# Mean and inverse deviation of each row made at the end of both zone stages, and read by the next stage

## The chip, the cores and the metric

The kernel runs on one core of a Trainium2 chip. The metric is the device time in microseconds (us) of one launch. Before the change it is 1563.74 us, the median of 3 runs (1562.68 to 1564.3). The profiled execution took 1563.83 us; its span, from the first to the last recorded instruction, is 1562.0 us.

## The reference

32 samples of 256 rows (tokens) with 128 features go through six steps. Each normalises the rows over their features, and adds its result to them:

```
x = x + 0.5 * zones(layernorm(x));  x = x + splat_attention(layernorm(x))
x = x + 0.5 * zones(layernorm(x));  x = x + 0.5 * splines(layernorm(x))
x = x + causal_attention(layernorm(x));  x = x + 0.5 * splines(layernorm(x))
layernorm(x) = (x - mean(x)) / sqrt(var(x) + 1e-5)        # over the 128 features of a row
zones(x)     = x + sum over 8 zones e of w[sample, e] * gelu(x @ Wa[e]) @ Wb[e]
               # w: softmax of a small router on the sample's mean row, the best 3 of 8 kept and rescaled
splines(x)   = (sum_h relu((x @ Win + bin) * W1 + b1) * W2 + b2) @ Wout + bout   # 64 knots, 16 bends each
```

The splat attention has 16 heads of 8 features and softmax over logits that come from 16 Gaussian centers per head. Only the layernorms that stand in front of the splat attention and of the first spline step bear on the change: their mean and 1 / sqrt(var + 1e-5) are two numbers for each row, known as soon as the zone step before has added its result to the row.

## The kernel before

All rows stay in SBUF for the whole launch, in `x_res`: 128 partitions, and for each sample two tiles (`TILES` = 2) of 128 features. The stages follow each other: a start with a first router (`route_a`), `zones_a`, `splat`, a second router (`route_b`), `zones_b`, `spline_a`, `causal`, `spline_b`. Each stage is a block of its own: one program for each engine, written by hand, with semaphores between them; the order of calls in such a program is the order on the engine. A stage begins when all engines have ended the one before (the barrier, L253, shows in the trace as `PEq L253`). Loops take two samples a turn (`pairs`), since buffers alternate.

**Moments of rows.** `RowNorm` (from L93) makes them for one sample in two parts. VectorE does `statistics` (L116 to L128): one `bn_stats` for each tile, then one `bn_aggr` for each, which leaves mean and variance in `moments`. GpSimd does `power` (L130 to L139): it adds eps, then raises to -0.5, which gives `rstd`. `s.mean` and `s.rstd` are tables in SBUF with one column for each tile of rows; stages can leave moments there for the next one. `PairNorm` (from L165) is the same for the two samples of a pair at once, used by the spline stages.

**Zone stages** (`zones`, L735 to L953). The incoming rows' moments are in the tables already. ScalarE normalises the rows (L865), TensorE turns them to features on partitions, ScalarE keeps the high float16 part and VectorE the low one (`keep_low`, L912 to L916). For each of the three chosen zones (k = 0 to 2) TensorE makes the first product (L804 to L806), ScalarE the gelu (L876), VectorE splits it in a high and a low float16 part (`split_unit`, L918 to L926), and TensorE makes the second product (L818 to L820). The sum over the three zones is copied by ScalarE and turned back by TensorE (L827). VectorE adds it to the rows (`add`, L928 to L933). GpSimd has added half of the normalised rows by then (`take_half`, L762 to L770: a product with 0.5 and a sum, 256 columns each). VectorE's order for one sample is this:

```
for k in range(TOP_K):
    split_unit(TOP_K * b + k, b, k)
if turns:
    keep_low(b + 2, parity)
if not is_first:
    add(b - 1, 1 - parity)
```

**Splat stage** (L956 to L1413). 32 samples in slots. It makes the moments of its own incoming rows in `statistics` (L1295 to L1298) on VectorE, four samples ahead, and `norm.power` and `apply` on GpSimd (L1376 to L1386), three ahead; `apply` subtracts the mean and multiplies by rstd. For the router and the zones that follow it also makes the moments of the rows that it has ended, with the same class (`ended`), and copies them into the tables (`keep_moments`, L1388 to L1392). VectorE's main work is the maxima of the logits (L1312).

**First spline stage** (`splines`, from L1417). 16 pairs of samples, 512 columns each. An engine's program is a list of steps with the number of pairs by which each is ahead, written by hand:

```
run(dve, (keep_inner, 1), (apply, 3), (statistics, 4), (add, -1))
run(pool, (bend, 1), (power, 4), (bias, 2))
run(act, (bend_first, 0), (keep_summed, -1), (bend_rest, 0), (keep_normed, 2))
```

`apply` normalises four tiles on VectorE, TensorE turns them (L1518) into `turned`, and `keep_normed` (L1556 to L1561) copies that out of PSUM on ScalarE. TensorE makes the knots' inputs (L1525, L1528), VectorE copies half of them (`keep_inner`, L1474) and bends some (L1477), ScalarE and GpSimd bend the rest, TensorE sums the bends of each knot (L1539), ScalarE copies the sums (`keep_summed`, L1578), and TensorE makes the result, which VectorE adds (L1485). The second spline stage calls the same function.

## Time and profile before

| | us |
|---|---|
| median of 3 runs (range) | 1563.74 (1562.68 to 1564.3) |
| profiled execution, whole | 1563.83 |
| its span | 1562.0 |
| TensorE busy | 1433.0 (92%) |
| VectorE busy | 1202.8 (77%) |
| ScalarE busy | 986.4 (63%) |
| GpSimd busy | 465.3 (30%) |

| stretch of the span | length | TensorE | VectorE | ScalarE | GpSimd |
|---|---|---|---|---|---|
| 61.90 to 331.00, zones_a | 269.10 | 266.88 | 216.97 | 162.49 | 53.28 |
| 335.00 to 917.00, splat | 582.00 | 565.58 | 451.47 | 370.46 | 136.99 |
| 961.00 to 1230.00, zones_b | 269.00 | 267.88 | 216.58 | 160.60 | 51.73 |
| 1231.60 to 1325.00, spline_a | 93.40 | 78.63 | 79.57 | 78.95 | 76.38 |

The times come from one profiled execution, those in the rows below in us from the span's start. PE is TensorE, DVE VectorE, ACT ScalarE, POOL GpSimd, SP SyncE; a "q" behind a name is the engine's sequencer. L with a number is a line of the kernel. An arrow reads "written <- read". In brackets stands how long the engine was idle before the instruction, and what it waited for. Busy shares are means over stages with different limits, so each stage is read by itself.

### The profile page before, as it was taken

How to read it: one execution, taken by the hardware profiler on the slowest of the kernel's cores; microseconds unless marked ns; L12 is line 12 of the kernel's file. 1: busy time of each engine (PE TensorE's matmuls, PEld its weight loads, DVE VectorE, ACT ScalarE, POOL GpSimd, SP SyncE). 2: the span in 40 equal slices, each digit the busy share in tenths (PEclk: the TensorE clock that was granted, in tenths of full speed). 3: DMA queues.
4: the chain of work that ended last, by engine and by line, in shares of the span. 5: the costliest groups of instructions: out<-in, count | busy, mean ns of one | idle time of the engine just before them, and what ended most of it. 6: DMA issues, size and time to landing. Idle time of an engine off the chain costs nothing. (4 is left out here: it accounts for less than half of the span.)

```text
span 1562.0 us, 43828 instructions
## 1 busy us (share of the span) xinstructions
PE 1433.0 (92%) x14442; PEld 1040.8 (67%) x14443; DVE 1202.8 (77%) x2634; ACT 986.4 (63%) x1478; POOL 465.3 (30%) x694
## 2 busy tenths in 40 slices
PE   1699999978999999999999987999999799799697
PEld 1499999955666666666666655999999544699443
DVE  8688888847778887877887854888888697587695
ACT  5366566534666666666666654665665399577597
POOL 6321221211222222222222202211221298222585
PEclk9999999988999999999999998999999899899899
DMA  5000000000000000000000000000000000000011
GB/s 237 1 1 0 0 0 0 0 1 1 2 2 2 1 0 0 0 0 0 0 0 1 2 2 2 1 0 0 0 0 0 1 0 1 1 0 1 8 47 54
DMA packets 9527, 14.40 MB, mean 9 GB/s; under 512 B 368, under 2 KB 8560, under 8 KB 8688
## 3 DMA queue, kind: packets, MB, share of 16 engines
q1 hardware_dynamic: 9456, 13.44, 2.3%
q8 instruction: 46, 0.75, 0.2%
q14 instruction: 25, 0.20, 0.0%
HBM read 9.25 MB, written 4.19 MB: 9 GB/s over the span
## 5 line engine op out<-in xcount | busy, mean ns | idle before, releaser
L1312 DVE TENSOR_REDUCE neg_max<-splat_fill_ps 128x2 f16<-128x512 f32 x512 | 334.0, 691 | 91.0 <-PE splat_fill_ps L1091 87.0
L1237 ACT ACTIVATE splat_probs<-splat_ring 128x1024 f32<-128x1024 f32 x256 | 248.1, 1021 | 98.3 <-PE splat_ring L1118 98.3
L876 ACT ACTIVATE zones_b_hidden<-zones_b_hidden_ps,gelu_scale 128x1024 f32<-128x1024 f32 x96 | 107.1, 1115 | 85.5 <-PE zones_b_hidden_ps L806 84.2
L876 ACT ACTIVATE zones_a_hidden<-zones_a_hidden_ps,gelu_scale 128x1024 f32<-128x1024 f32 x96 | 107.1, 1115 | 84.8 <-PE zones_a_hidden_ps L806 83.5
L1118 PE MATMUL splat_ring<-splat_queries,splat_keys 32*128 32x256 f32 x2048 | 153.0, 393 | 4.2 <-ACT splat_probs L1237 3.2
L1091 PE MATMUL splat_fill_ps<-splat_keys,splat_queries 32*128 32x256 bf16 x1024 | 146.0, 278 | 6.2 <-DVE neg_max L1312 3.3
L1132 PE MATMUL splat_mixed_ps<-splat_probs,values 128*32 128x256 f32 x2048 | 137.0, 385 | 0.4 <-ACT splat_probs L1237 0.4
L925 DVE SCALAR_TENSOR_TENSOR zones_b_hid_lo<-zones_b_hidden,unit_scale,zones_b_hid_hi 128x1024 f16<-128x1024 f32 x96 | 123.6, 1288 | 3.4
L925 DVE SCALAR_TENSOR_TENSOR zones_a_hid_lo<-zones_a_hidden,unit_scale,zones_a_hid_hi 128x1024 f16<-128x1024 f32 x96 | 123.6, 1288 | 3.4
L133 POOL TENSOR_TENSOR splat_ended_shifted<-splat_ended_moments,eps 128x2 f32<-128x2 f32 x32 | 6.3, 197 | 344.4 <-DVE splat_ended_moments L127 344.4
L1118 PEld LDWEIGHTS splat_ring<-splat_queries,splat_keys 32*128 32x128 f32 x2048 | 100.0, 185 | 11.6 <-ACT splat_probs L1237 4.4
L804 PE MATMUL zones_b_hidden_ps<-zones_b_norm_hi,wa_hi 128*128 128x256 f16 x384 | 105.8, 276 | 0.3 <-DVE zones_b_norm_lo L915 0.3
L804 PE MATMUL zones_a_hidden_ps<-zones_a_norm_hi,wa_hi 128*128 128x256 f16 x384 | 105.5, 275 | 0.3 <-DVE zones_a_norm_lo L915 0.3
L805 PE MATMUL zones_b_hidden_ps<-zones_b_norm_lo,wa_hi 128*128 128x256 f16 x384 | 105.8, 275 | 0.0
L806 PE MATMUL zones_b_hidden_ps<-zones_b_norm_hi,wa_lo 128*128 128x256 f16 x384 | 105.7, 275 | 0.0
L818 PE MATMUL zones_a_result_ps<-zones_a_hid_hi,wb_hi 128*128 128x256 f16 x384 | 104.7, 273 | 1.0 <-DVE zones_a_hid_lo L925 1.0
L805 PE MATMUL zones_a_hidden_ps<-zones_a_norm_lo,wa_hi 128*128 128x256 f16 x384 | 105.4, 275 | 0.0
L806 PE MATMUL zones_a_hidden_ps<-zones_a_norm_hi,wa_lo 128*128 128x256 f16 x384 | 105.4, 275 | 0.0
L818 PE MATMUL zones_b_result_ps<-zones_b_hid_hi,wb_hi 128*128 128x256 f16 x384 | 104.7, 273 | 0.6 <-DVE zones_b_hid_lo L925 0.6
L819 PE MATMUL zones_a_result_ps<-zones_a_hid_lo,wb_hi 128*128 128x256 f16 x384 | 104.7, 273 | 0.0
L820 PE MATMUL zones_a_result_ps<-zones_a_hid_hi,wb_lo 128*128 128x256 f16 x384 | 104.7, 273 | 0.0
L819 PE MATMUL zones_b_result_ps<-zones_b_hid_lo,wb_hi 128*128 128x256 f16 x384 | 104.7, 273 | 0.0
(356 smaller groups left out, 3498.3 us busy)
## 6 DMA issues: line engine op xcount, KB each, us to landing
x_res<-rows SPq DMA_DIRECT2D x4, 1024.0 KB, 18.8
out<-x_res SPq DMA_DIRECT2D x16, 256.0 KB, 2.3
stage_a<-wa SPq DMA_DIRECT2D x1, 2048.0 KB, 8.8
stage_b<-wb SPq DMA_DIRECT2D x1, 2048.0 KB, 13.2
packed<-table SPq DMA_DIRECT2D x1, 840.0 KB, 4.4
```

Source lines behind the costliest of these rows:

```text
L804: nc.tensor.matmul(out, s.wa_hi[:, at], x_hi, start=True, stop=False)
L805: nc.tensor.matmul(out, s.wa_hi[:, at], x_lo, start=False, stop=False)
L806: last = nc.tensor.matmul(out, s.wa_lo[:, at], x_hi, start=False, stop=True)
L818: nc.tensor.matmul(out, s.wb_hi[:, at], hi, start=(k == 0 and c == 0), stop=False)
L819: nc.tensor.matmul(out, s.wb_hi[:, at], lo, start=False, stop=False)
L876: nc.scalar.activation(hidden[k][:, :, :], hidden_ps[of][:, :, :], ACT.Gelu_apprx_tanh, scale=s.gelu_scale[:, :]).then_inc(gelu_done, 1)
L925: nc.vector.scalar_tensor_tensor(hid_lo[k][:, :, :], hidden[k][:, :, :], scale, hid_hi[k][:, :, :], ALU.mult, ALU.subtract).then_inc(split, 1)
L1091: last = nc.tensor.matmul(fill_ps[f % 2][:, n, :], upper(queries[at], rows, t + n, slice(tile * P, (tile + 1) * P)), upper(keys[at], rows, ...
L1118: last = nc.tensor.matmul(ring[g // 2][:, 2 * (g % 2) + key_tile, :], keys[at][rows, t, key_tile * P:(key_tile + 1) * P], queries[at][rows ...
L1132: last = nc.tensor.matmul(mixed_ps[head_rows(g), t % 2, :], s.values[:, at, key_tile, HEAD_GROUPS * t + g, :], probs[(2 * t + g // 2) % PR ...
L1237: nc.scalar.activation(probs[u % PROB_BUFFERS][:, :, :, :].rearrange("p h k i -> p (h k) i"), ring[u % 2][:, :, :], ACT.Exp).then_inc(exp_ ...
L1312: nc.vector.tensor_reduce(s.neg_max[:, tile, t:t + 2, GROUP * g + SPLATS], fill_ps[f % 2][:, :, :], AX.X, ALU.max, negate=True).then_inc(m ...
```

## The change

Both zone stages now make the moments of the rows that they have ended. On VectorE each sample b from the third on gets the statistics of sample b - 2 (`end`), between `keep_low` and `add`. GpSimd makes their power and copies mean and rstd into the tables (`keep_moments`), four samples behind, after each halving; the first six halvings stand outside the loop. Behind the last add VectorE does `end` for the last two samples, and GpSimd's last four `keep_moments` follow its last halving. The splat stage loses its own `statistics` and `norm.power`; its `apply` reads the tables. The first spline stage loses `statistics` and `power`; its `apply` reads the tables, one column a tile, and `keep_normed` moves from ScalarE to VectorE. The second spline stage stays as it is.

```diff
-def zones(nc, s, stage):
+def zones(nc, s, stage, moments=False):
...
+        ended = RowNorm(nc, s, ctx, stage + "_ended", 0)
...
-                take_half(0, 0)
-                take_half(1, 1)
-                with pairs(pool, 2, SAMPLES) as i:
+                def keep_moments(b, parity):
+                    ended.power(pool, b, parity)
+                    columns = slice(TILES * b, TILES * (b + 1)) if isinstance(b, int) else bass.ds(b * TILES, TILES)
+                    settle(pool, ended.rstd_ready, b + 1)
+                    nc.gpsimd.tensor_copy(s.mean[:, columns], ended.moments[parity][:, :, 0])
+                    nc.gpsimd.tensor_copy(s.rstd[:, columns], ended.rstd[parity][:, :]).then_inc(ended.ready, 1)
+                for b in range(4):
+                    take_half(b, b % 2)
+                take_half(4, 0)
+                if moments:
+                    keep_moments(0, 0)
+                take_half(5, 1)
+                if moments:
+                    keep_moments(1, 1)
+                with pairs(pool, 6, SAMPLES) as i:
                     for parity in range(2):
                         take_half(i + parity, parity)
+                        if moments:
+                            keep_moments(i + parity - 4, parity)
+                if moments:
+                    for b in range(SAMPLES - 4, SAMPLES):
+                        keep_moments(b, b % 2)
...
+                    if moments and not (isinstance(b, int) and b < 2):
+                        end(b - 2, parity)
                     if not is_first:
                         add(b - 1, 1 - parity)
+                def end(b, parity):
+                    settle(dve, added, b + 1)
+                    settle(dve, ended.ready, b - 1)
+                    ended.statistics(dve, b, parity)
                 keep_low(0, 0)
                 keep_low(1, 1)
                 sample(0, 0, is_first=True)
-                with pairs(dve, 1, LOOP_END) as i:
+                for b in range(1, 5):
+                    sample(b, b % 2)
+                with pairs(dve, 5, LOOP_END) as i:
                     sample(i, 1)
                     sample(i + 1, 0)
                 sample(SAMPLES - 3, 1)
                 sample(SAMPLES - 2, 0, turns=False)
                 sample(SAMPLES - 1, 1, turns=False)
                 add(SAMPLES - 1, 1)
+                if moments:
+                    end(SAMPLES - 2, 0)
+                    end(SAMPLES - 1, 1)
...
-        norm = RowNorm(nc, s, ctx, stage, 1, DEEP)
         ended = RowNorm(nc, s, ctx, stage + "_ended", 0, DEEP)
-        normed, norm_ready = norm.out[0], norm.ready
+        normed, norm_ready = sb(stage + "_normed", [P, TILES, P], F32), sem("norm_ready")
...
-                def statistics(b, at):
-
-                    wait(dve, norm_ready, b - DEEP + 1)
-                    norm.statistics(dve, b, at)
...
-                    if there(b, 4):
-                        statistics(b + 4, after)
...
-                def apply(b, at):
-                    pool.wait_ge(norm.rstd_ready, b + 1)
-                    wait(pool, norm_ready, b)
+                def apply(b):
+                    columns = slice(TILES * b, TILES * (b + 1)) if isinstance(b, int) else bass.ds(b * TILES, TILES)
+                    settle(pool, norm_ready, b)
                     nc.gpsimd.tensor_tensor(centered[:, :, :], tile_of(s.x_res, b),
-                                            norm.moments[at][:, :, 0:1].to_broadcast([P, TILES, P]),
+                                            s.mean[:, columns].unsqueeze(2).to_broadcast([P, TILES, P]),
                                             ALU.subtract).then_inc(centered_ready, 1)
-                    pool.wait_ge(centered_ready, b + 1)
-                    wait(pool, normt_done, b)
+                    settle(pool, centered_ready, b + 1)
+                    settle(pool, normt_done, b)
                     nc.gpsimd.tensor_tensor(normed[:, :, :], centered[:, :, :],
-                                            norm.rstd[at][:, :].unsqueeze(2).to_broadcast([P, TILES, P]),
+                                            s.rstd[:, columns].unsqueeze(2).to_broadcast([P, TILES, P]),
                                             ALU.mult).then_inc(norm_ready, 1)
...
-                        norm.power(pool, b + 3, at)
-                        apply(b + 3, at)
+                        apply(b + 3)
...
+def splines(nc, s, stage, out=None, normed_before=False):
...
-                    norm.apply(dve, p, parity, normed[parity])
+                    if normed_before:
+                        for t in range(PAIR):
+                            column = bass.ds(p * PAIR + t, 1)
+                            last = nc.vector.tensor_scalar(normed[parity][:, t, :], pair_of(s.x_res, p, t),
+                                                           s.mean[:, column], s.rstd[:, column],
+                                                           ALU.subtract, ALU.mult)
+                        last.then_inc(norm_ready, 1)
+                    else:
+                        norm.apply(dve, p, parity, normed[parity])
+                def keep_normed(p, parity):
+                    dve.wait_ge(turned_ready, p + 1)
+                    wait(dve, inner_a_ready, p - 1)
+                    nc.vector.tensor_copy(normed_t[parity][:, :], turned[:, :]).then_inc(normt_ready, 1)
...
-                run(dve, (keep_inner, 1), (apply, 3), (statistics, 4), (add, -1))
+                if normed_before:
+                    run(dve, (keep_inner, 1), (keep_normed, 2), (apply, 3), (add, -1))
+                else:
+                    run(dve, (keep_inner, 1), (apply, 3), (statistics, 4), (add, -1))
...
-                run(pool, (bend, 1), (power, 4), (bias, 2))
+                if normed_before:
+                    run(pool, (bend, 1), (bias, 2))
+                else:
+                    run(pool, (bend, 1), (power, 4), (bias, 2))
...
-                run(act, (bend_first, 0), (keep_summed, -1), (bend_rest, 0), (keep_normed, 2))
+                if normed_before:
+                    run(act, (bend_first, 0), (keep_summed, -1), (bend_rest, 0))
+                else:
+                    run(act, (bend_first, 0), (keep_summed, -1), (bend_rest, 0), (keep_normed, 2))
...
-        zones(nc, s, "zones_a")
+        zones(nc, s, "zones_a", moments=True)
         recycle(nc)
         splat_attention(nc, s, "splat")
         route(nc, s, "route_b")
-        zones(nc, s, "zones_b")
+        zones(nc, s, "zones_b", moments=True)
         recycle(nc)
-        splines(nc, s, "spline_a")
+        splines(nc, s, "spline_a", normed_before=True)
```

In the pieces of the instruction order below, `ISA` and `REGISTER_ALU` are instructions of the engine's sequencer (waits, addresses), and brackets give the semaphores waited for.

**VectorE, loop over samples in zones_a.** Before, from the low part of the unit k = 2 (`hid_lo`) to the add:

```order
L925 SCALAR_TENSOR_TENSOR zones_a_hid_lo<-zones_a_hidden,unit_scale,zones_a_hid_hi 128x1024 [waits zones_a_high]
L914 REGISTER_ALU
L915 TENSOR_TENSOR zones_a_norm_lo<-zones_a_turned,zones_a_norm_hi 128x256 [waits zones_a_norm_high]
L932 ISA [waits zones_a_x_ready,zones_a_turned_ready]
L932 TENSOR_TENSOR x_res<-x_res,zones_a_result_ps 128x256
```

After, from `norm_lo` on (the low part of unit k = 2 stands ahead of it as before):

```order
L936 TENSOR_TENSOR zones_a_norm_lo<-zones_a_turned,zones_a_norm_hi 128x256 [waits zones_a_norm_high]
L71 REGISTER_ALU
L71 REGISTER_ALU [waits zones_a_added]
L63 REGISTER_ALU [waits zones_a_ended_norm_ready]
L120 ISA [waits zones_a_ended_moments_ready]
L120 BN_STATS zones_a_ended_stats<-x_res 128x6
L120 ISA
L120 BN_STATS zones_a_ended_stats<-x_res 128x6
L127 BN_AGGR zones_a_ended_moments<-zones_a_ended_stats 128x2 [waits zones_a_ended_stats_ready]
L127 BN_AGGR zones_a_ended_moments<-zones_a_ended_stats 128x2
L953 ISA [waits zones_a_x_ready,zones_a_turned_ready]
L953 TENSOR_TENSOR x_res<-x_res,zones_a_result_ps 128x256
```

Two `BN_STATS`, two `BN_AGGR` and the waits for `added` and `ended_norm_ready` have come between `norm_lo` and the add to `x_res`.

**GpSimd, loop over samples in zones_a.** Before, one halving and the next:

```order
L774 ISA
L766 TENSOR_TENSOR zones_a_half<-zones_a_normed,half 128x256 [waits zones_a_x_ready,zones_a_norm_ready]
L770 ISA [waits zones_a_half_ready]
L770 TENSOR_TENSOR x_res<-x_res,zones_a_half 128x256
```

After, from the add of one halving to the add of the next, for the second sample of a turn:

```order
L133 TENSOR_TENSOR zones_a_ended_shifted<-zones_a_ended_moments,eps 128x2 [waits zones_a_ended_rstd_ready]
L63 REGISTER_ALU [waits zones_a_ended_shifted_ready]
L137 TENSOR_TENSOR zones_a_ended_rstd<-zones_a_ended_shifted,minus_half 128x2 [waits zones_a_ended_norm_ready]
L778 ISA [waits zones_a_ended_rstd_ready]
L778 COPY mean<-zones_a_ended_moments 128x2
L779 REGISTER_ALU
L779 COPY rstd<-zones_a_ended_rstd 128x2
L766 REGISTER_ALU
L768 TENSOR_TENSOR zones_a_half<-zones_a_normed,half 128x256 [waits zones_a_x_ready,zones_a_norm_ready]
L772 ISA [waits zones_a_half_ready]
L772 TENSOR_TENSOR x_res<-x_res,zones_a_half 128x256
```

Two operations on two columns, with a wait for VectorE's `ended_moments`, and two copies into the tables now stand between two halvings.

**VectorE, start of spline_a.** Before, the first pair's moments, its norm (x3 stands for three more rows alike), and the second pair's:

```order
L183 BN_STATS spline_a_stats<-x_res 128x6 x4
L189 BN_AGGR spline_a_moments<-spline_a_stats 128x2 [waits start_zone_stats_ready]
L189 BN_AGGR spline_a_moments<-spline_a_stats 128x2 x3
L205 TENSOR_SCALAR spline_a_normed<-x_res,spline_a_moments,spline_a_rstd 128x128 [waits start_zone_powered]
L205 TENSOR_SCALAR spline_a_normed<-x_res,spline_a_moments,spline_a_rstd 128x128 x3
L183 BN_STATS spline_a_stats<-x_res 128x6 [waits start_zone_moments_ready]
```

After:

```order
L1495 TENSOR_SCALAR spline_a_normed<-x_res,mean,rstd 128x128 x4
L1505 COPY spline_a_normed_t<-spline_a_turned 128x512 [waits start_packed_loaded]
L1495 TENSOR_SCALAR spline_a_normed<-x_res,mean,rstd 128x128 x4
L1513 COPY spline_a_inner_b<-spline_a_inner_b_ps 128x512 [waits start_masks_ready]
L1516 TENSOR_SCALAR spline_a_bent<-spline_a_inner_b,packed,minus_bias 128x512 [waits start_blank]
L1505 COPY spline_a_normed_t<-spline_a_turned 128x512 [waits start_packed_loaded]
```

The statistics are gone, the norm of the first pair is the stage's first instruction, and the copy of the turned rows (L1505) stands between the norms.

## Rows read from the trace of the kernel before

**Rows 1.** busy time in zones_a: start:end and length, then each engine's busy us (xcount)

```profile
61.90:331.00 269.10, 266.88 (x2418) 238.84 (x2418) 216.97 (x255) 162.49 (x224) 53.28 (x64) 1.00 0.00 0
```

**Rows 2.** timeline, zones_a: start us, length us, engine line op out<-in xcount [idle before]

```profile
91.92 0.42 DVE L932 TENSOR_TENSOR x_res<-x_res,zones_a_result_ps 128x256 f32 x1 [0.82 <-PE zones_a_result_ps L827]
92.55 0.75 DVE L922 TENSOR_SCALAR zones_a_hid_hi<-zones_a_hidden,unit_scale 128x1024 f16<-128x1024 f32 x1 [0.21 <-issue]
93.34 1.28 DVE L925 SCALAR_TENSOR_TENSOR zones_a_hid_lo<-zones_a_hidden,unit_scale,zones_a_hid_hi 128x1024 f16<-128x1024 f32 x1
...
95.53 0.27 PE L818 MATMUL zones_a_result_ps<-zones_a_hid_hi,wb_hi 128*128 128x256 f16 x1
...
98.98 0.42 DVE L915 TENSOR_TENSOR zones_a_norm_lo<-zones_a_turned,zones_a_norm_hi 128x256 f16<-128x256 f32 x1
100.24 0.42 DVE L932 TENSOR_TENSOR x_res<-x_res,zones_a_result_ps 128x256 f32 x1 [0.84 <-PE zones_a_result_ps L827]
```

**Rows 3.** timeline of DVE and POOL: three meetings of the two engines

```profile
97.78 1.28 DVE L925 SCALAR_TENSOR_TENSOR zones_a_hid_lo<-zones_a_hidden,unit_scale,zones_a_hid_hi 128x1024 f16<-128x1024 f32 x1
...
98.57 0.97 POOL L766 TENSOR_TENSOR zones_a_half<-zones_a_normed,half 128x256 f32<-128x256 f32 x1 [6.34 <-ACT zones_a_normed L865]
...
75.35 1.24 POOL L770 TENSOR_TENSOR x_res<-x_res,zones_a_half 128x256 f32 x1 [0.26 <-POOL zones_a_half L766]
76.05 1.63 DVE L925 SCALAR_TENSOR_TENSOR zones_a_hid_lo<-zones_a_hidden,unit_scale,zones_a_hid_hi 128x1024 f16<-128x1024 f32 x1
...
1246.82 1.03 POOL L199 TENSOR_TENSOR spline_a_rstd<-spline_a_shifted,minus_half 128x4 f32<-128x4 f32 x1
1247.15 0.55 DVE L1477 TENSOR_SCALAR spline_a_bent<-spline_a_inner_b,packed,minus_bias 128x512 f32<-128x512 f32 x1
```

**Rows 4.** timeline, splat slot, DVE then POOL: moments of ended rows

```profile
621.03 0.49 DVE L120 BATCH_NORM_STATS2 splat_ended_stats<-x_res 128x6 f32 x2
621.62 0.25 DVE L127 BATCH_NORM_AGGREGATE splat_ended_moments<-splat_ended_stats 128x2 f32<-128x6 f32 x2
621.79 1.26 DVE L1312 TENSOR_REDUCE neg_max<-splat_fill_ps 128x2 f16<-128x512 f32 x2
624.80 1.30 DVE L1312 TENSOR_REDUCE neg_max<-splat_fill_ps 128x2 f16<-128x512 f32 x2 [1.75 <-PE splat_fill_ps L1091]
...
621.95 0.20 POOL L133 TENSOR_TENSOR splat_ended_shifted<-splat_ended_moments,eps 128x2 f32<-128x2 f32 x1 [11.09 <-DVE splat_ended_moments L127]
...
623.27 0.19 POOL L1392 COPY rstd<-splat_ended_rstd 128x2 f32 x1
```

**Rows 5.** timeline, border from zones_a to splat

```profile
333.68 0.42 DVE L932 TENSOR_TENSOR x_res<-x_res,zones_a_result_ps 128x256 f32<-128x256 f32 x1 [2.31 <-PE zones_a_result_ps L827]
335.23 0.49 DVE L120 BATCH_NORM_STATS2 splat_stats<-x_res 128x6 f32<-128x128 f32 x2 [1.13 <-PEq L253]
...
337.55 0.61 POOL L1379 TENSOR_TENSOR splat_centered<-x_res,splat_moments 128x256 f32<-128x256 f32 x1
```

**Rows 6.** timeline, start of spline_a

```profile
1231.62 0.87 DVE L183 BATCH_NORM_STATS2 spline_a_stats<-x_res 128x6 f32<-128x128 f32 x4 [1.15 <-PEq L253]
...
1234.40 1.12 DVE L205 TENSOR_SCALAR spline_a_normed<-x_res,spline_a_moments,spline_a_rstd 128x128 f32<-128x128 f32 x4 [1.42 <-POOL spline_a_rstd L199]
...
1236.72 0.60 ACT L1560 ACTIVATE spline_a_normed_t<-spline_a_turned 128x512 f32<-128x512 f32 x1 [7.20 <-PE spline_a_turned L1518]
...
1238.19 1.12 DVE L205 TENSOR_SCALAR spline_a_normed<-x_res,spline_a_moments,spline_a_rstd 128x128 f32<-128x128 f32 x4 [1.40 <-POOL spline_a_rstd L199]
...
1246.42 0.69 DVE L1474 COPY spline_a_inner_b<-spline_a_inner_b_ps 128x512 f32<-128x512 f32 x1
```

**Rows 7.** timeline of ACT, spline_a: the copies of the knots' sums

```profile
1316.07 0.69 ACT L1578 ACTIVATE spline_a_summed<-spline_a_summed_ps,packed 128x512 f32<-128x512 f32 x1 [0.22 <-PE spline_a_summed_ps L1539]
...
1321.54 0.69 ACT L1578 ACTIVATE spline_a_summed<-spline_a_summed_ps,packed 128x512 f32<-128x512 f32 x1 [0.22 <-PE spline_a_summed_ps L1539]
...
1327.01 0.69 ACT L1578 ACTIVATE spline_a_summed<-spline_a_summed_ps,packed 128x512 f32<-128x512 f32 x1 [0.71 <-PE spline_a_summed_ps L1539]
```

## Prediction: what the change does to the time

> **What bounds the kernel now.** I read the busy time by stage first, then the timelines of one steady sample or pair in each touched stage, then the four borders between stages.
>
> In the zone stages TensorE is the bound: 266.88 of 269.10 us busy in zones_a [rows 1]. VectorE has air there. One sample is 8.32 us long (add to add, 91.92 to 100.24), and before every add VectorE stands idle for 0.82 to 0.84 us, waiting for the result that TensorE turns back [rows 2]. The new work is put into this hole. The next high part of a loop's first sample begins 0.63 after the add (0.21 of it issue); its first low part ends at 94.62 and TensorE asks for it at 95.53, so VectorE may be 0.91 late before TensorE notices [rows 2].
>
> In the splat stage the statistics sit where VectorE is early: two maxima after them it is idle for 1.75 us until TensorE has filled the next [rows 4]. Taking 0.84 us away in front of that idle time makes it longer and nothing else.
>
> In the spline stage the period is not set by ScalarE's sum of work. The copies of the knots' sums start at 1316.07, 1321.54 and 1327.01: two gaps of 5.47 us. The first of these pairs still had the copy of turned rows on ScalarE, the second (near the end, where no pair is left to turn) had not; only the idle time in front of the sums' copy grew, from 0.22 to 0.71 us [rows 7]. The loop that closes is bend, TensorE's knot sums, their copy, bend; the copy that the change moves to VectorE is not in it.
>
> **The change part by part.**
>
> *Statistics in the zone loops (+).* Word for word the splat stage does the same: two statistics, 0.59 later two aggregations, 0.17 after these the next instruction starts [rows 4]. Behind the low part of the norm (0.42, of which the last 0.08 overlap, as 97.78 to 98.98 for a 1.28 instruction shows [rows 2, 3]) that gives 0.34 + 0.59 + 0.17 = 1.10 us until the add may start. Today it is 100.24 - 98.98 = 1.26. So the work fits into the wait, with 0.16 over. The four register instructions ahead of the statistics stand in the same form in the splat loop; I count them as hidden behind the 0.42 instruction, at most 0.1 if not.
>
> *VectorE's whole sample.* Three units of a high part (0.79 to the next start) and a low part (1.20): 5.97. With 1.10 and the step from add to high part, 0.63 or 0.34 (0.42 less 0.08), a sample is 7.70 or 7.41, in the mean 7.56, against 8.32: 0.76 free.
>
> *GpSimd is pushed into VectorE's way (+).* This is the dear part. GpSimd halves the norm and adds it to the rows; today it starts at 98.57, under the last low part, waits until that ends at 99.06 and is done 0.48 later, while VectorE does things that don't mind [rows 2, 3]. Now the moments of four samples back stand in front of the next halving in its program, and these wait for VectorE's aggregation. GpSimd needs 1.59 us for moments (621.87 to 623.46) [rows 4], so the halving starts some 1.6 us after the aggregation, which is under the first low part, and the two operations fall beside the unit k = 1. They collide: a GpSimd add that began at 75.35 ran to 76.59, and the low part begun at 76.05 took 1.63 instead of 1.28 [rows 3], so 0.54 of overlap cost 0.35; 0.19 are free. The halving ends 0.48 after the low part before, the high part begins 0.08 before that end: overlap 0.56, cost 0.37. The add meets the next low part as in the row: 0.35. Together 0.72, and VectorE's sample is 8.28 against TensorE's 8.32. It stays hidden, by 0.04 us a sample and the 0.91 us of head start. Bounds: nothing (the collisions fall into VectorE's waits for gelu), and 0.2 more (the register instructions and the two copies of moments, 0.19 each). The power of the moments I take at nothing: GpSimd's power of 1.03 at 1246.82 ran over a whole VectorE instruction at 1247.15 that kept its 0.55 us [rows 3]. Term: 0, bounds 0 and 3.6 per stage.
>
> A sentence of the Trainium skill speaks against this. SBUF — State Buffer, section Who interferes with whom, has any GpSimd instruction and a VectorE instruction in a two-port mode exclude each other for the whole instruction. The long pair (75.35 against 76.05) agrees; the short one (1246.82 against 1247.15) does not. What the rule would make of the time is the third rival.
>
> *End of each zone stage (+).* The last two samples have nothing to hide in. After the last add (333.68, 0.42 [rows 5]) VectorE does the moments of sample 30 in 0.34 + 0.59 + 0.25 = 1.18 from the add's start, 0.76 beyond its end. Then GpSimd does two passes, 1.59 and 1.51 (the second is queued, its 0.08 of signal gone): 3.86 us, during which sample 31's statistics run along. Nothing else works then, and the barrier waits for it. Twice: +7.72. Bounds 3.1 and 4.5 each (a pass less its copies; another 0.6 for signals).
>
> *Start of the splat stage (-).* Today the first statistics start at 335.23 and GpSimd's subtraction at 337.55 [rows 5]; the subtraction now comes first: -2.32. Each later sample's own moments hide already.
>
> *Start of the first spline stage (-).* Before, the first norm starts 2.78 after the stage's first instruction and the second at 6.57 (1231.62, 1234.40, 1238.19) [rows 6]. Now the first starts at once and ends at 1.12; the transposes reach the copying engine 1.20 later (1235.52 to 1236.72) [rows 6]; the copy, now VectorE's, takes 0.69 like its other copy of 512 columns out of PSUM [rows 6], less 0.08; the second norm starts at 2.93. From there the chain is as before: -3.64. Bounds -2.9 and -4.4.
>
> *Steady spline pairs.* VectorE loses statistics and gains 0.69; TensorE, whose chain runs through the copy, gets it from an engine that waits for it. The pair stays at 5.47: 0. If the copy came too late it would show as a longer pair: VectorE needs a copy, a bend, a copy and a norm, 0.69 + 0.55 + 0.69 + 1.12 = 3.05 us [rows 3, 6], before TensorE can turn the next rows and make the product that the next round starts on. That leaves 2.4 us for TensorE; turning alone took 1.20 with its signals at the stage's start [rows 6].
>
> *Sum.* 7.72 - 2.32 - 3.64 + 0 = +1.76 on the profiled execution's 1563.83 us, so 1565.6; the median of the timed runs lies 0.09 lower, so 1565.5.
>
> **Rivals.**
>
> *Slower: VectorE becomes the bound of the zone stages.* One mechanism: GpSimd's displaced halving and add block VectorE's unit k = 1. It decides from 0.76 us a sample on, and I have 0.72. For it: the narrow sum, and that both operations are queued behind the same instruction. Against: where VectorE waits for gelu part of it is absorbed. With 0.1 more than counted a sample lasts 8.38, and 28 samples lose 1.7 less the head start of 0.91, 1.5 us over both stages: 1567. With 0.2 more, 8.48: 28 x 0.16 - 0.91 = 3.6 a stage, 1572.7.
>
> *Faster: the relieved engines were bounds after all.* If ScalarE's sum of work set the spline pair, 16 times the 0.49 that its copy takes of a pair (0.71 less 0.22 of idle time [rows 7]) would go: 7.8, so 1557.8. A VectorE bound in the splat stage would give up to 32 x 0.84 = 27 us, 1539. Against both stand the equal gaps of 5.47 [rows 7] and the idle 1.75 [rows 4]. I see nothing for it but that both engines are busy.
>
> *Much slower: even short GpSimd instructions lock VectorE out.* The power of two columns (about 0.7 in this form, between the rows of 621.95 and 623.27) would hold up the first high part for some 0.6, the copies 0.15: 0.72 + 0.75 = 1.47, a sample of 9.03, 28 x 0.71 - 0.91 = 19 a stage, 1604. By the rule of the Trainium skill quoted above this would be the case. The undisturbed 0.55 us of [rows 3] speaks against it.
>
> **How the numbers follow.** Forecast (zone loops hidden, borders as summed) 0.57, with a range of its own of 1563.5 to 1567.5; VectorE bound 0.28; faster 0.11; lock of short instructions 0.04. 0.2% is 3.1 us and about what a measurement of this kernel can tell from no change, so "same" is 1560.6 to 1566.9. Of the forecast's case some 0.1 lies beyond, of the slower case nearly all: slower 0.39, same 0.50, faster 0.11. The range goes from 1560.5 to 1573.
>
> **What would show it.** In the zone loops: the wait before the add nearly gone, the add still about 1.2 after the norm's low part, some high and low parts of unit k = 1 at 1.1 and 1.6 us, the sample still 8.3. A sample of 8.4 or more with TensorE idle before its second products is the slower rival. At the end of each zone stage VectorE's two pairs of statistics and two GpSimd passes, 3.9 us. First transposes of the splat stage 1.3 to 1.5 us after its first instruction, slots as long as before with VectorE's idle time longer. In the spline stage the second norm near 2.9, pairs of 5.47 with ScalarE idle 0.7 before each copy of sums. I am wrong if pairs or slots change their length, or the borders cost less than 3 us each.

## The result and the profile after

The changed kernel takes 1575.12 us (median of 4 runs, 1573.86 to 1576.46) against 1563.62 (4 runs, 1562.68 to 1564.3) of the kernel before: ratio 1.0073, 95% interval 1.006 to 1.0085. It is slower by 11.5 us. The forecast was 1565.5 with a range up to 1573, so the time lies above the range. The profiled execution took 1574.54 us, its span is 1572.8.

Stretch by stretch, in us, read from VectorE's adds and each stage's first instruction; "again" are second traces of the same two kernels, taken later (e12 and e11 below):

| stretch | before | again | after | again | change, first traces | forecast |
|---|---|---|---|---|---|---|
| zones_a, first to last add | 250.03 | 250.03 | 253.96 | 253.99 | +3.93 | 0 |
| zones_b, first to last add | 250.04 | 250.04 | 253.53 | 253.59 | +3.49 | 0 |
| last add of zones_a to splat | 1.55 | 1.55 | 5.07 | 5.08 | +3.52 | +3.86 |
| last add of zones_b to spline_a | 1.56 | 1.57 | 5.07 | 5.07 | +3.51 | +3.86 |
| splat, first instruction to first add | 75.29 | 76.55 | 74.73 | 72.97 | -0.56 | -2.32 |
| spline_a, whole | 105.08 | 103.80 | 100.52 | 101.73 | -4.56 | -3.64 |
| spline_b (not changed), first instruction to last add | 102.78 | 102.49 | 104.08 | 102.71 | +1.30 | 0 |

The rest moves by 0.1 us in sum in the first traces. The ends of the zone stages came out roughly as forecast; the starts of splat and spline_a vary from trace to trace and are taken up below. The zone stages did not come out as forecast: 7.4 us where nothing was expected.

Busy time in the stretch of zones_a that [rows 1] shows of before (start:end and length, then PE, PEld, DVE, ACT, POOL busy us):

```profile
61.90:331.00 269.10, 265.74 (x2389) 235.08 (x2390) 250.34 (x368) 161.67 (x223) 138.68 (x180) 1.00 0.00 0
```

VectorE went from 216.97 to 250.34 us and GpSimd from 53.28 to 138.68: more than 29 samples of added work by the rows of [rows 4] come to (0.74 us each on VectorE, 21; some 1.3 on GpSimd, 38). Where it goes is seen in one steady sample, which answers to [rows 2, 3]. Timeline of zones_a after, VectorE, then GpSimd:

```profile
255.39 0.74 DVE L943 TENSOR_SCALAR zones_a_hid_hi<-zones_a_hidden,unit_scale 128x1024 f16<-128x1024 f32 x1
256.17 1.66 DVE L946 SCALAR_TENSOR_TENSOR zones_a_hid_lo<-zones_a_hidden,unit_scale,zones_a_hid_hi 128x1024 f16<-128x1024 f32 x1
257.75 1.21 DVE L943 TENSOR_SCALAR zones_a_hid_hi<-zones_a_hidden,unit_scale 128x1024 f16<-128x1024 f32 x1
259.00 1.28 DVE L946 SCALAR_TENSOR_TENSOR zones_a_hid_lo<-zones_a_hidden,unit_scale,zones_a_hid_hi 128x1024 f16<-128x1024 f32 x1
260.20 0.42 DVE L936 TENSOR_TENSOR zones_a_norm_lo<-zones_a_turned,zones_a_norm_hi 128x256 f16<-128x256 f32 x1
260.53 0.48 DVE L120 BATCH_NORM_STATS2 zones_a_ended_stats<-x_res 128x6 f32 x2
261.11 0.25 DVE L127 BATCH_NORM_AGGREGATE zones_a_ended_moments<-zones_a_ended_stats 128x2 f32<-128x6 f32 x2
261.37 0.42 DVE L953 TENSOR_TENSOR x_res<-x_res,zones_a_result_ps 128x256 f32 x1
262.09 0.75 DVE L943 TENSOR_SCALAR zones_a_hid_hi<-zones_a_hidden,unit_scale 128x1024 f16<-128x1024 f32 x1 [0.30 <-issue]
...
270.06 0.42 DVE L953 TENSOR_TENSOR x_res<-x_res,zones_a_result_ps 128x256 f32 x1
...
254.42 1.09 POOL L778 COPY mean<-zones_a_ended_moments 128x2 f32 x1 [0.23 <-POOL zones_a_ended_rstd L137]
255.46 0.72 POOL L779 COPY rstd<-zones_a_ended_rstd 128x2 f32 x1
256.14 0.61 POOL L768 TENSOR_TENSOR zones_a_half<-zones_a_normed,half 128x256 f32<-128x256 f32 x1
257.01 1.40 POOL L772 TENSOR_TENSOR x_res<-x_res,zones_a_half 128x256 f32 x1 [0.26 <-POOL zones_a_half L768]
...
261.88 1.00 POOL L137 TENSOR_TENSOR zones_a_ended_rstd<-zones_a_ended_shifted,minus_half 128x2 f32<-128x2 f32 x1 [0.16 <-POOL zones_a_ended_shifted L133]
```

No VectorE row of the sample shows a wait for another engine: every instruction follows the last, and from add to add it is 8.69 us (261.37 to 270.06). The next sample takes 8.30, without the 0.30 of issue at the loop's top. The mean of the two is 8.495; before, the samples alternate between 8.31 and 8.28, in the mean 8.295. TensorE now waits for VectorE's low part. This is its only line in the view of waits from 100 to 300 us (us in all, times, longest); in the kernel before that window shows no wait of TensorE at all:

```profile
PE zones_a_result_ps L839 <- DVE zones_a_hid_lo L946: 2.0, 9, 0.2
```

What makes the sample long are two meetings with GpSimd. The halving (256.14) makes the low part of unit k = 1 last 1.66 instead of 1.28; its add (257.01) makes the high part of unit k = 2 last 1.21 instead of 0.75. And the two copies of two columns, 0.19 us each in [rows 4], take 1.09 and 0.72: the first ends at 255.51, with the low part that began at 254.19 and lasted 1.28, the second at 256.18, with the high part (255.39 + 0.74). So by their times GpSimd's smallest copies waited for VectorE to finish, and the halving behind them got one unit later.

The border, answering to [rows 5]:

```profile
337.48 0.42 DVE L953 TENSOR_TENSOR x_res<-x_res,zones_a_result_ps 128x256 f32<-128x256 f32 x1 [1.59 <-PE zones_a_result_ps L848]
...
338.73 0.19 POOL L133 TENSOR_TENSOR zones_a_ended_shifted<-zones_a_ended_moments,eps 128x2 f32<-128x2 f32 x1 [1.72 <-DVE zones_a_ended_moments L127]
...
340.03 0.19 POOL L133 TENSOR_TENSOR zones_a_ended_shifted<-zones_a_ended_moments,eps 128x2 f32<-128x2 f32 x1
...
341.18 0.18 POOL L779 COPY rstd<-zones_a_ended_rstd 128x2 f32<-128x2 f32 x1
342.55 0.61 POOL L1405 TENSOR_TENSOR splat_centered<-x_res,mean 128x256 f32<-128x256 f32 x1 [1.19 <-SPq L1064]
```

Two passes of GpSimd, 1.30 us from one to the next, begin 0.83 after the end of the last add; the subtraction is now splat's first instruction. Splat's slot, answering to [rows 4], and spline_a, answering to [rows 6, 7]:

```profile
626.93 0.48 DVE L120 BATCH_NORM_STATS2 splat_ended_stats<-x_res 128x6 f32 x2
627.52 0.25 DVE L127 BATCH_NORM_AGGREGATE splat_ended_moments<-splat_ended_stats 128x2 f32<-128x6 f32 x2
628.11 1.29 DVE L1340 TENSOR_REDUCE neg_max<-splat_fill_ps 128x2 f16<-128x512 f32 x2 [0.35 <-PE splat_fill_ps L1124]
631.54 1.89 DVE L1340 TENSOR_REDUCE neg_max<-splat_fill_ps 128x2 f16<-128x512 f32 x3 [2.13 <-PE splat_fill_ps L1124]
...
1245.27 1.11 DVE L1495 TENSOR_SCALAR spline_a_normed<-x_res,mean,rstd 128x128 f32<-128x128 f32 x4 [2.93 <-PEq L253]
1247.58 0.69 DVE L1505 COPY spline_a_normed_t<-spline_a_turned 128x512 f32<-128x512 f32 x1 [1.21 <-PE spline_a_turned L1563]
1248.19 1.10 DVE L1495 TENSOR_SCALAR spline_a_normed<-x_res,mean,rstd 128x128 f32<-128x128 f32 x4
...
1315.45 0.69 ACT L1623 ACTIVATE spline_a_summed<-spline_a_summed_ps,packed 128x512 f32<-128x512 f32 x1 [0.70 <-PE spline_a_summed_ps L1584]
1320.93 0.69 ACT L1623 ACTIVATE spline_a_summed<-spline_a_summed_ps,packed 128x512 f32<-128x512 f32 x1 [0.70 <-PE spline_a_summed_ps L1584]
```

In splat VectorE's idle time grew to 0.35 and 2.13; the first 27 steps from add to add take 17.9 to 18.3 us, as before. In spline_a the second norm starts 2.92 after the first (forecast 2.93). The copies of the sums follow each other at 5.48 and 5.56 us in turn (before 5.47 and 5.55), with ScalarE idle 0.70 or 0.78 ahead of each.

### The profile page after: what moved, and what is told of

Same layout as the page of the kernel before. It is cut to its first block and busy times, and to the rows that moved or that the text cites. A ratio compares the mean times of both kernels' runs of the same rounds, so it can differ in the third digit from the quotient of the medians.

```text
span 1572.8 us, 44337 instructions
## 1 busy us (share of the span) xinstructions
PE 1439.0 (91%) x14442; PEld 1040.1 (66%) x14443; DVE 1237.7 (79%) x2650; ACT 980.2 (62%) x1462; POOL 594.1 (38%) x854
## 5 line engine op out<-in xcount | busy, mean ns | idle before, releaser
L946 DVE SCALAR_TENSOR_TENSOR zones_a_hid_lo<-zones_a_hidden,unit_scale,zones_a_hid_hi 128x1024 f16<-128x1024 f32 x96 | 133.6, 1391 | 3.4
L946 DVE SCALAR_TENSOR_TENSOR zones_b_hid_lo<-zones_b_hidden,unit_scale,zones_b_hid_hi 128x1024 f16<-128x1024 f32 x96 | 133.6, 1391 | 3.4
L841 PE MATMUL zones_b_result_ps<-zones_b_hid_hi,wb_lo 128*128 128x256 f16 x384 | 104.7, 273 | 0.0
```

Of the source, the lines that this page charges most:

```text
L841: last = nc.tensor.matmul(out, s.wb_lo[:, at], hi, start=False, stop=(k == TOP_K - 1 and c == CHUNKS - 1))
L946: nc.vector.scalar_tensor_tensor(hid_lo[k][:, :, :], hidden[k][:, :, :], scale, hid_hi[k][:, :, :], ALU.mult, ALU.subtract).then_inc(split, 1)
```

## The experiments

Theory: GpSimd's displaced halving and add stretch VectorE's units; that alone makes VectorE the bound of the zone stages. Rivals: the statistics themselves fill VectorE; or the cost lies elsewhere. A second question is where splat's 1.8 us went that were missing from the forecast.

**e1, the makers alone.** Zones as changed, `splat_attention` and `splines` as before.

```diff
-        splines(nc, s, "spline_a", normed_before=True)
+        splines(nc, s, "spline_a")
```

> Both zone stages make the moments as in the changed kernel, but splat and the first spline stage still make their own and read nothing of them. Theory (collisions of GpSimd's displaced halving with VectorE make VectorE the bound of the zone stages, and the two ends cost 3.5 us each): zone stages +3.9 and +3.5 between first and last add, ends +3.5 each, and if the longer idle time at the end is what makes TensorE start splat at a low clock for longer, another 1.9 in splat before its first add: 1563.6 + 16.3 = 1580. Rival for splat's 1.9 us (it comes from how splat reads the tables): the way from splat's first maximum to its first add is as in the kernel before, 59.8 us, and the time is 1578.

Measured: 1576.58 us (ratio 1.0084, 1.0071 to 1.0098). Zone stages +3.94 and +2.70, ends +3.54 and +3.53. Splat's first add comes 75.26 after its first instruction, as before, although 5.09 us lay between the last add of zones_a and that first instruction. From splat's first maximum to its first add it is 59.9, the rival's 59.8. My theory for splat's loss (the longer idle time makes it slower through a lower clock) falls. The mean granted clock over the 75.26 us was indeed lower, 0.80 against 0.84, yet the stretch was no longer; the mean clock alone doesn't set its length.

**e2, the readers alone.** The zone stages make no moments.

```diff
-        zones(nc, s, "zones_a", moments=True)
+        zones(nc, s, "zones_a", moments=False)
...
-        zones(nc, s, "zones_b", moments=True)
+        zones(nc, s, "zones_b", moments=False)
```

> The zone stages make no moments (they are left out), splat and the first spline stage read the tables, which hold the moments of older rows: the readers' part alone. Theory: splat starts 2.4 us earlier, spline_a gains 3.3 at its start, nothing steady changes, and splat's way from first maximum to first add is 59.8 us as before, since the border's idle time is again short: 1563.6 - 5.7 = 1557.9. Rival (splat's 1.9 us come from reading the tables): 61.7 us there, 1559.8. Rival of the prediction (ScalarE's copy was a bound of the spline pairs): pairs under 5.47 us and below 1555.

Measured: 1557.87 us (0.9969, 0.9958 to 0.998), the time that the theory gave. Zone stages 250.18 and 250.17. Splat's first add at 74.12. From first maximum to first add it is 61.7, though, which was the sign of the rival (reading the tables costs 1.9 us); e11 and e12 take this up. The makers cost 13.0 and the readers bring 5.8, so 7.2 is what the two add up to; the change has 11.5. The first traces put 0.6 of what lies between into zones_b, where every other sample takes 8.66 in the change and 8.57 in e1. Most of the rest stands in three places that vary between two traces of one kernel (below): 1.8 in spline_a (1.3 of it a long last pair in the trace of before), 1.6 in spline_b and 0.6 at splat's start. Whether the medians differ for the same reason stays open.

**e3, moments kept five samples behind.** In GpSimd's program the halving comes ahead of the wait for VectorE's aggregation. Its first eight halvings stand outside the loop, and five samples' moments are left for the end.

```diff
-                            keep_moments(i + parity - 4, parity)
+                            keep_moments(i + parity - 5, 1 - parity)
```

> The changed kernel with GpSimd keeping moments five samples behind instead of four, so that the halving no longer stands behind the wait for VectorE's aggregation. Theory (the collisions of the displaced halving are the whole 7.4 us of the zone stages): high and low parts of the units k = 1 and 2 back to 0.75 and 1.28 us, idle time before VectorE's units again, samples 8.28 to 8.32, zone stages 250.1 from first to last add, 1575.1 - 7.4 = 1567.7. Rival (the statistics and their register instructions fill VectorE by themselves, or the power and copies collide wherever they stand): samples stay at a mean of 8.4 or more, 1572 to 1576.

Measured: 1567.05 us (1.0024, 1.0013 to 1.0034), 8.1 below the change. Both zone stages 250.18. The same statistics, powers and copies are there; only the halving's place is another. Timeline of zones_a, VectorE, then GpSimd:

```profile
262.91 0.75 DVE L939 TENSOR_SCALAR zones_a_hid_hi<-zones_a_hidden,unit_scale 128x1024 f16<-128x1024 f32 x1 [0.29 <-ACT zones_a_hidden L893]
263.70 1.28 DVE L942 SCALAR_TENSOR_TENSOR zones_a_hid_lo<-zones_a_hidden,unit_scale,zones_a_hid_hi 128x1024 f16<-128x1024 f32 x1
...
259.59 1.10 POOL L778 COPY mean<-zones_a_ended_moments 128x2 f32 x1 [0.23 <-POOL zones_a_ended_rstd L137]
260.62 0.72 POOL L779 COPY rstd<-zones_a_ended_rstd 128x2 f32 x1
264.48 0.97 POOL L768 TENSOR_TENSOR zones_a_half<-zones_a_normed,half 128x256 f32<-128x256 f32 x1 [3.13 <-ACT zones_a_normed L882]
265.72 0.73 POOL L772 TENSOR_TENSOR x_res<-x_res,zones_a_half 128x256 f32 x1 [0.27 <-POOL zones_a_half L768]
```

VectorE waits for gelu again, its units are 0.75 and 1.28 again. The halving begins under the low part and waits that one out, as in [rows 3]. In this sample the copies still take 1.10 and 0.72, in the next one 0.57 and 0.18, and they cost VectorE nothing in either. This settles the zone stages.

**e5, the last two samples handed over.** Their moments are made at the next stage's start instead of behind the last add; the rest as changed.

```diff
-                    end(SAMPLES - 2, 0)
-                    end(SAMPLES - 1, 1)
...
+                for n in range(2):
+                    late.statistics(dve, n, n, SAMPLES - 2 + n)
```

The new statistics stand ahead of VectorE's slots in splat. GpSimd makes their power and copies (`keep_late`) behind its first `apply` there; spline_a does the same for its last pair.

> The changed kernel with only the last two samples' moments handed to the next stage; GpSimd keeps four samples behind as in the change. Theory (ends and collisions add up independently): 1575.1 - 7.0 for the two ends - 0.8 that splat's start gains when the idle time before it is short = 1567.3; zone stages still 253.5 to 254.0 between first and last add. Rival (the ends overlap something, so that handing over is worth less without the other mend): above 1569.

Measured: 1566.03 us (1.002, 1.0011 to 1.0029). Ends 1.57 and 1.63, zone stages 253.95 and 253.52: the ends are worth their 7.0, and nothing of them hid the zones' loss. The median lies 9.1 below the change; in the traces 1.8 more are won at splat's start (72.95), which the edit need not have caused (e11).

**e4, both mends.**

> As e3_five_back, and the moments of the last two samples are no longer made behind the last add but at the start of the next stage, where VectorE and GpSimd wait for TensorE. Theory: both ends fall back to about 1.55 us from last add to the next stage's first instruction (-7.0), and splat's start loses no clock (-1.9): 1567.7 - 8.9 = 1558.8, faster than before by 4.8. Rival (splat's 1.9 us come from reading the tables): 1560.7. Rival (the late moments delay the first samples there): splat's first maximum more than 13.1 us after its first instruction, or spline_a's first add more than 19.7, and 1560 to 1563.

Measured: 1559.32 us (0.9977, 0.9967 to 0.9988): faster than before. Zone stages 250.19 and 250.18, ends 1.57 and 1.62. The late moments cost nothing: splat's first maximum 12.41 and spline_a's first add 19.54 after the first instruction.

**e7, e4 with the copy of turned rows back on ScalarE.**

```diff
-                    run(dve, (keep_inner, 1), (keep_normed, 2), (apply, 3), (add, -1))
+                    run(dve, (keep_inner, 1), (apply, 3), (add, -1))
```

> As e4_five_back_handed, with the copy of turned rows in spline_a back on ScalarE. Theory (the pair's period is set by the loop through bend, TensorE's knot sums and their copy): the period stays at 5.47 us, spline_a's first add within 0.3 us of e4's, and the time within 1 us of 1559.3. Rival (the move was worth something in the steady pairs or at the start): 0.3 us or more a pair or 1.5 us at the start, 1561 to 1566.

Measured: 1557.37 us (0.9964, 0.995 to 0.9978), the fastest version; against e4's interval the difference of 2 us is not certain. In the trace the copies of the sums still follow each other at 5.47 and 5.55, but the start differs from what I expected:

```profile
1229.36 2.14 DVE L1506 TENSOR_SCALAR spline_a_normed<-x_res,mean,rstd 128x128 f32<-128x128 f32 x8 [1.21 <-PEq L253]
```

With no copy of its own to wait for, VectorE makes both first norms in one go. The first add comes 18.19 instead of 19.54 after the first instruction; the whole stage is 99.66 instead of 100.31. No other trace that reads the tables has its first add before 19.19 (e2).

**e6, without GpSimd's two copies in the zone stages.** The tables keep older moments.

```diff
-                    nc.gpsimd.tensor_copy(s.mean[:, columns], ended.moments[parity][:, :, 0])
-                    nc.gpsimd.tensor_copy(s.rstd[:, columns], ended.rstd[parity][:, :]).then_inc(ended.ready, 1)
```

> The changed kernel without GpSimd's two copies of moments in the zone stages (left out, so the tables hold older moments). In the changed kernel these copies last 1.10 and 0.72 us instead of 0.19 each beside VectorE, and so move the halving to beside the units k = 1 and 2. Theory (it is the halving and its add that cost VectorE 0.83 us a sample, wherever they meet a unit): they now meet the units k = 0 and 1, cost between 0.7 and 0.83, and a sample is 8.37 to 8.50 in the mean. Rival (the place alone is wrong, and as costed in the prediction a halving that comes right behind the power is hidden): 8.28 to 8.32 a sample. The ends get 0.6 shorter each (3.5 to 2.9). 1572 by the theory, 1566 by the rival.

Measured: 1568.08 us (1.0037, 1.0026 to 1.0048). Samples of 8.24 and 8.55, in the mean 8.395; zone stages +1.89 and +1.48; ends 4.51 and 4.53. The collisions now are one unit earlier, at k = 0 and 1:

```profile
260.96 1.51 DVE L944 SCALAR_TENSOR_TENSOR zones_a_hid_lo<-zones_a_hidden,unit_scale,zones_a_hid_hi 128x1024 f16<-128x1024 f32 x1
262.40 1.21 DVE L941 TENSOR_SCALAR zones_a_hid_hi<-zones_a_hidden,unit_scale 128x1024 f16<-128x1024 f32 x1
...
260.64 0.76 POOL L769 TENSOR_TENSOR zones_a_half<-zones_a_normed,half 128x256 f32<-128x256 f32 x1
261.65 1.41 POOL L773 TENSOR_TENSOR x_res<-x_res,zones_a_half 128x256 f32 x1 [0.26 <-POOL zones_a_half L769]
```

It costs 0.23 + 0.46 = 0.69 here (0.32 + 0.46 = 0.78 in the next sample), near the size that was forecast (0.72). But the pairs are others: the halving costs the low part, and GpSimd's add the next high part, where the prediction had the halving delay the high part of k = 1 and the add its low part. And even so the stage is longer. About half of the zones' loss is left without the copies; the other half came with them, most likely because they move the halving one unit on, since in e3 they cost VectorE nothing by themselves.

**e8 and e13, more statistics on VectorE.** e3 with bn_stats and bn_aggr done once more (e8) and three times more (e13) into spare tiles.

```diff
+                    for t in range(TILES):
+                        nc.vector.bn_stats(again_stats[:, t, :], tile_of(s.x_res, b, t))
+                    for t in range(TILES):
+                        nc.vector.bn_aggr(again_moments[:, t, :], again_seed[:, t, :])
```

> As e3_five_back, with every bn_stats and bn_aggr of the zone stages' loops done a second time into spare tiles (not used). It measures how far VectorE is from being the bound once the collisions are gone. Theory (VectorE's sample is 8.30 + 0.39/2 less the 0.83 of collisions, 7.67): with 0.84 more it is 8.50, so samples of 8.50 in the mean, 5.7 us more a zone stage and 1.6 more at the ends: 1580. Rival (some 8.3 us of VectorE's sample are taken already, hidden in waits that the statistics need): every added 0.84 shows in full, 9.1 a sample and over 1600.

Measured: 1566.22 us (1.0018, 1.0009 to 1.0028), the same as e3, zone stages 250.17 and 250.18. Both expectations missed: I had priced the pair at 0.84, which holds the wait between statistics and aggregation; the extra pair has no such wait and puts 0.51 us between the real ones and the add. So the dose was too small to reach the bound, and the time shows that VectorE had at least that much room.

> As e3_five_back, with the statistics of the zone stages' loops made three more times instead of once as in e8 (not used). In e8 the extra pair of statistics and aggregations put 0.51 us between the real ones and the add, and left VectorE idle for 0.6 us in 16.6, so its sample was 8.0 us. Theory (VectorE's sample is a plain sum and decides from 8.3 on): with two more it is 8.0 + 1.02 = 9.0 us, so samples of 9.0 in the mean and zone stages some 20 us longer each: 1607. Rival (TensorE paces the stage whatever VectorE does, and waits for gelu absorb more): samples under 8.6, below 1585.

Measured: 1603.9 us (1.0262, 1.0232 to 1.0292); samples of 8.89 us, all alike:

```profile
270.91 0.46 DVE L974 BATCH_NORM_STATS2 zones_a_again_stats<-x_res 128x6 f32 x2
271.28 0.24 DVE L976 BATCH_NORM_AGGREGATE zones_a_again_moments<-zones_a_again_seed 128x2 f32<-128x6 f32 x2
271.43 0.39 DVE L953 TENSOR_TENSOR x_res<-x_res,zones_a_result_ps 128x256 f32 x1
...
280.33 0.39 DVE L953 TENSOR_TENSOR x_res<-x_res,zones_a_result_ps 128x256 f32 x1
```

VectorE is a plain sum once it is the bound: 8.89 less 3 x 0.51 is 7.36 without the extra statistics (with the register instructions at the loop's top hidden; in the change it is 8.495 - 0.84 = 7.66 with them). Either lies 0.6 or more below TensorE's 8.3: the room for the statistics was there, and the collisions took it. Here GpSimd's copies begin beside VectorE's add and take 0.18 or 0.19.

**e9, first sample of splat late.** e4 with `keep_late` ahead of splat's first `apply`.

> As e4_five_back_handed, but at splat's start GpSimd makes the late moments of samples 30 and 31 before it normalises sample 0 instead of after, so that TensorE gets its first rows some 3.9 us later (first maximum at 16.3 us instead of 12.4 after the stage's first instruction). Theory A (an earlier first sample is partly given back, since TensorE then does its first slots at 1.2 GHz for longer): first add only 0.5 to 2.5 us later than in e4 (73.96 after the stage's first instruction), 1560 to 1562. Theory B (what readers gave back at splat's start has nothing to do with how early they start): first add 3.9 us later, 1563.2.

Measured: 1563.74 us (0.9999, 0.9989 to 1.0009). GpSimd's first subtraction starts 3.64 after the stage's first instruction, the first maximum is at 17.06 and the first add at 77.01, 3.05 later than e4's 73.96. This doesn't decide. The first maximum is 4.65 later than in e4, and 1.6 of that is gone by the first add; but from first maximum to first add two traces of one kernel also differ by 1.7 and 1.9 (below). The median, 4.4 above e4's, is nearer to theory B (an earlier start is kept), yet of the 5.9 us between the two traces 3.2 lie in spline_a, which the edit leaves alone.

**e11 and e12, both kernels once more.**

> The changed kernel once more, for a second trace. Zone stages +3.9 and +3.5, ends +3.5 each again; what is not of the change moves: spline_b's last pair 5.5 instead of 6.8 us (its TensorE fell to the lower clock there in the first trace), and splat from its first instruction to its last maximum between 583.8 and 585.5 us, the spread of the eight traces in which it reads the tables.

> The kernel before once more, for a second trace. Splat from its first instruction to its last maximum 586.0 us as in the first trace and in e1; spline_a's last pair 5.5 instead of 6.75 us if the lower clock there was chance, 6.75 if it belongs to the kernel.

Measured: the change 1576.47 us (2 runs; 1.0082, 1.0062 to 1.0103), before 1563.54. Zones and ends repeat within 0.1 us (table above). What does not repeat is splat's start. TensorE's granted clock stands in the third number from the end of these windows, each from splat's first instruction to its first add; before, before again, the change, the change again:

```profile
335.23:410.52 75.29, 61.94 (x645) 36.15 (x646) 45.99 (x96) 34.48 (x44) 15.80 (x26) 0.84 0.01 1
```
```profile
335.20:411.75 76.55, 63.53 (x645) 37.15 (x646) 45.88 (x95) 34.58 (x44) 15.79 (x26) 0.80 0.00 1
```
```profile
342.55:417.28 74.73, 63.93 (x645) 37.49 (x646) 42.06 (x71) 34.63 (x44) 11.32 (x16) 0.79 0.00 1
```
```profile
342.90:415.87 72.97, 61.95 (x645) 36.16 (x646) 42.08 (x71) 34.47 (x44) 11.34 (x16) 0.84 0.00 1
```

With the same 645 matmuls one kernel needs 75.29 or 76.55, the other 74.73 or 72.97, longer each time the mean clock is 0.80 or 0.79 instead of 0.84, with the matmuls busy for 63.5 and 63.9 us instead of 61.9. The difference lies between the first maximum and the first add: 59.8 and 61.5 before, 61.7 and 59.8 in the change. Both lengths occur with and without the tables, so the rival of e2 is out. Three traces with their own statistics (before twice, e1) have a mean of 75.70, the ten that read the tables and start at once (the change twice, e2 to e8, e13) 73.82: the readers gain 1.9, against 2.32 forecast, and the first pair of traces hid most of it. My expectation of e12 (586.0 to the last maximum) missed too, with 587.4. spline_a's last pair was 5.47 instead of 6.75, so the long one was chance, and so was spline_b's in the change (5.47 again in e11). The traces of e3, e8 and e9 have a long one too, of 6.8 to 7.1 us.

## Why the prediction was wrong

*What bounds the zone stages: right for before, wrong for after.* The step that failed is "GpSimd is pushed into VectorE's way", whose term was 0 because 8.28 stood below 8.32. Its mechanism, the displaced halving and add colliding with VectorE's units, was right in kind. The margin was smaller than it looked: 8.32 is the longer of two samples in turn (8.31 and 8.28, in the mean 8.295), so 0.015 was left, not 0.04. Measured, VectorE's sample is 8.495 in the mean (8.69 and 8.30). Of the 0.215 between, 0.12 are the collisions (0.38 + 0.46 = 0.84, not 0.72), 0.07 the statistics' way to the add (260.20 to 261.37, 1.17 instead of 1.10), 0.045 the loop's top (0.72 instead of 0.63, every other sample); these make 0.235, and 0.02 is rounding. Such a margin could not carry three such errors. e6 shows that even collisions of the size that I had costed run over it. That their sum came near 0.72 is in part luck, as which instruction holds up which was forecast wrongly (e6).

*The bound of the copies was wrong.* I gave them 0.19 each as in splat and at most 0.2 in sum; beside VectorE's units they took 1.09 and 0.72. By themselves they cost VectorE nothing (e3), but with them the collisions stand at the units k = 1 and 2 and cost 0.84, without them at k = 0 and 1 and cost about 0.74 (e6).

*The slower rival came true.* "VectorE becomes the bound of the zone stages", with 0.2 more a sample: 8.48 and 3.6 a stage, 1572.7. Measured 8.495, 3.9 and 3.5. It had 0.28; with a margin of 0.04 on a sum of a dozen terms it deserved at least as much as the forecast. Of the 2.4 us from 1572.7 to 1575.1, the first trace shows 1.3 in spline_b and the second 3.1 between splat's first add and the first of zones_b, where the step from the 29th to the 30th add takes 17.8 instead of 16.2 us. The code is the same in both kernels there; the granted clock was 0.86 in the second trace from 915 to 990 us, and 0.93 in the first. Why the median holds as much stays open.

*Ends: right.* 3.5 each instead of 3.86, since a pass of GpSimd that nothing disturbs takes 1.30 instead of 1.59 and 1.51.

*Splat's start: right in sign,* 1.9 instead of 2.32, with 1.3 to 1.8 between two traces of one kernel. Slots unchanged: right.

*spline_a: right in place, too large in size.* Second norm at 2.92, as forecast, and the pairs as long as before. But "from there the chain is as before" was only partly so: the second copy of sums stands at 23.95 after the stage's first instruction in both traces of before, and at 20.54 and 21.88 in those of the change. The stage gains 2.1 to 3.3 once the last pair of before is set to its usual 5.47 (103.80 less 101.73 and 100.52), against 3.64 with a lower bound of 2.9. The faster rival (ScalarE's copy bounds the pair) is out, by e7. That the copy's move costs something at the start was not seen.

*The rule on the lock.* The Trainium skill (SBUF — State Buffer, Who interferes with whom) has GpSimd and a VectorE instruction in a two-port mode exclude each other for its whole length, and counts `tensor_scalar` (here the high part) among those that can run in one. GpSimd's second copy agrees with it: it ends with a high part. VectorE in its turn kept its 0.75 beside GpSimd's power (262.09, beside a power from 261.88 to 262.88), which does not agree, so the third rival, 1604, did not come. The sentence says nothing of the low part, a `scalar_tensor_tensor`; the prediction's long pair (75.35 against 76.05) was with a low part and so bears on it less than the prediction had it.

## What to carry to other kernels

Work put into an engine's wait costs what it pushes on the other engines' programs. Before adding a wait to an engine, look at what stands behind it in its queue and what that will then run beside. Here one number (five samples behind instead of four) gave back 8 us, and moments that are due at a stage's end belong into the next stage's start, where engines wait anyway: 7 us. A forecast that a term stays hidden by 0.04 us in 8.3 is no better than even, and the sample that it is measured against must be a mean: here two lengths alternated, 0.03 apart.

## What the runs showed of the hardware

- A GpSimd copy of two columns, 0.18 us alone, took up to 1.27 beside VectorE's high and low parts, and ended with one of them, without slowing them (e3).
- A GpSimd halving of 256 columns (0.61 us undisturbed) that began 0.03 before a low part made that 0.38 longer. GpSimd's add, begun under a low part, waited for its end, and the high part due at that end was 0.46 longer; a halving begun under a low part likewise waited for its end, and where the subtraction `norm_lo` followed (before and e3), that kept its 0.42.
- The time from splat's first instruction to its first add moved by 1.3 and 1.8 us between two traces of one kernel, with TensorE's mean granted clock 0.79 or 0.80 in the longer and 0.84 in the shorter. A third kernel (e1) had 0.80 in a stretch as long as the shorter one of before, so what decides it was not settled.
